# Graph attention on one core: windows of 128 nodes that begin at a group's first target, with the running maximum and sums kept for the window alone and scattered to memory

## The reference, cut to what matters

```python
z = h @ W.T
e = leaky_relu((z @ w1)[src] + (z @ w2)[dst], 0.01)
m = segment_max(e, dst)
num = exp(e - m[dst])
den = segment_sum(num, dst)
w_e = rel_emb[etype] * num / den[dst]
h_agg = segment_sum(w_e[:, None] * z[src], dst)
x = layernorm(x + h_agg + bias_w)
```

## Time and profile before

| | us |
|---|---|
| median of 3 runs (lowest, highest) | 9428.82 (9421.71, 9435.07) |
| profiled execution, device time | 9424.09 |
| its span | 9422.5 |
| attention stage, first to last row_scale (line 1046) | 3241.9 to 5041.8 |

### The profile page before, as it was taken

One profiled execution on the slowest core, in us unless ns is written; L12 is line 12 of the kernel. 1 busy time (PEld: TensorE's weight loads), 2 busy tenths in 40 slices (PEclk: granted clock), 3 DMA queues, 4 the chain that ended last, 5 costly groups with the idle time before them and its releaser, 6 DMA issues. The chain is left out here.

```text
span 9422.5 us, 155371 instructions
## 1 busy us (share of the span) xinstructions
PE 7624.8 (81%) x38400; PEld 4762.1 (51%) x38401; DVE 4037.7 (43%) x9289; ACT 3255.1 (35%) x5403; POOL 5567.4 (59%) x5492
## 2 busy tenths in 40 slices
PE   1998888888888576666667999999999888888886
PEld 1554444444444366555554444444444655566664
DVE  5887777774444366666654110000011332332333
ACT  4012334565555476666552000000000332332332
POOL 4888788877777010000003666676766677777775
PEclk6999999999999766666667999999999999999998
DMA  4233445566666443333325999999998322322222
GB/s 121 75 105 123 150 162 177 201 231 219 212 223 224 160 145 129 118 112 106 99 93 197 332 322 345 337 334 337 330 339 289 94 78 76 78 78 78 78 77 67
DMA packets 563155, 1661.17 MB, mean 176 GB/s; under 512 B 115314, under 2 KB 312030, under 8 KB 519495
## 3 DMA queue, kind: packets, MB, share of 16 engines
q1 hardware_dynamic: 352666, 1182.75, 35.8%
q0 software_dynamic: 206976, 473.99, 16.9%
q10 hardware_dynamic: 3312, 1.94, 0.1%
HBM read 1174.46 MB, written 483.82 MB: 176 GB/s over the span
## 5 line engine op out<-in xcount | busy, mean ns | idle before, releaser
L913 PE MATMUL wide<-ring 128*128 128x392 bf16 x14112 | 2501.0, 339 | 496.2 <-DVE ring L843 259.5
L520 POOL DMA_INDIRECT z_got<-z_table,z_idx x1568 | 2113.4, 1348 | 597.6 <-issue 430.2
L913 PEld LDWEIGHTS wide<-ring 128*128 128x128 bf16 x14112 | 1408.5, 100 | 1588.5 <-issue 820.9
L1672 POOL DMA_INDIRECT sorted_recs<-dn_rec_in,type_f x1568 | 1512.1, 964 | 735.2 <-issue 444.9
L1763 POOL DMA_INDIRECT l_rows<-h_table,l_recs x1568 | 1558.6, 994 | 520.1 <-issue 477.5
L1487 PE MATMUL wide<-stream,X 128*128 128x512 f32 (+1 forms) x2548 | 1048.1, 571 | 23.5 <-DVE X L1613 17.8
L1046 POOL TENSOR_TENSOR row_scale<-rows,rel 128x8 f32<-128x8 f32 x196 | 38.9, 198 | 1451.2 <-ACT m_scale L1150 1451.2
L1206 PE MATMUL wide<-rows,onehot 128*128 128x130 f32 x3904 | 845.0, 403 | 42.7 <-issue 21.1
L373 PE MATMUL wide<-l_rows,l_onehot 128*128 128x128 f32 x3904 | 579.3, 310 | 366.6 <-DVE X L386 366.6
L1206 PEld LDWEIGHTS wide<-rows,onehot 128*128 128x128 f32 x3904 | 788.0, 308 | 91.8 <-issue 91.5
L1862 DVE TENSOR_TENSOR l_rows<-l_filters,l_rows 128x1024 f32<-128x1024 f32 x196 | 240.3, 1226 | 1327.9 <-DMA l_rows<-h_table,l_recs 1310.5
(11 more groups left out here) (262 smaller groups left out, 8640.2 us busy)
## 6 DMA issues: line engine op xcount, KB each, us to landing
stream<-w_dense SPq DMA_DIRECT2D x252, 1792.0 KB, 9.5
stream<-c_dense SPq DMA_DIRECT2D x84, 1792.0 KB, 9.2
z_edges<-z_got POOLq DMA_DIRECT2D x196, 528.0 KB
rows<-z_edges POOLq DMA_DIRECT2D x196, 528.0 KB
dst_bc<-in_dst_row SPq DMA_DIRECT2D x196, 512.0 KB, 3.6
c_dense<-A SPq DMA_DIRECT2D x49, 1568.0 KB
w_dense<-A SPq DMA_DIRECT2D x49, 1568.0 KB
c_dense<-H SPq DMA_DIRECT2D x49, 1568.0 KB
```

The source lines that it names most:

```text
L520: e.indirect_dma_start(out=z_got[:, s, t, :], out_offset=None, in_=z_table, in_offset=bass.IndirectOffsetOnAxis(ap=z_idx[:, s, t:t + 1], a ...
L913: ins = e.matmul(banks[:, bass.ds(to[v], 1), int(m > 0), 0:WC].rearrange("p a x -> p (a x)"), lhsT=slots[:, k, m * P:(m + 1) * P], rhs=slo ...
L1672: e.indirect_dma_start(out=sorted_recs, out_offset=bass.IndirectOffsetOnAxis(ap=pos_i[:, g * TILES + t:g * TILES + t + 1], axis=0), in_=re ...
```

## The change

A group's window now begins at its first target `lo` and holds the nodes lo to lo + 127, node n still on partition n mod 128. The partitions below `lo mod 128` then stand for nodes of the next block. The end of a group's range becomes first + ((largest - lo + 128) >> 7).

- The prelude also stores each group's `lo` and broadcasts it to all partitions (`lo_f`); from it come the masks `below` and `above`.
- `node_tab` holds for each block the node's far value, its own score and the score's three parts. GpSimd (`describe`), two groups ahead, builds a window's record in `win` from two neighbouring blocks of it, and `W_RESET`, which is negative and huge where the node on a partition changes from one window to the next.
- VectorE keeps the maximum in `max_was` and the sums in `kept`, one column and one row of 130 values a partition. The steps of both are exponentiated into `m_scale`, twice as wide as before.
- After each `add_pair` GpSimd (`put_sums`) scatters `kept` by an indirect DMA to `agg_dram`, at rows made from the window's far value. VectorE adds to `kept` again only when that scatter has landed (`s_kept`).
- `agg_dram` is filled with zeros at the start on ScalarE's queue, which also loads `iota` now. The targets `dst_f` are turned into keys on VectorE.
- The dense stage loads `A0` from `agg_dram` by 7 DMAs on SyncE's queue ahead of its first stream load, and takes `rden` and `rdeg` slice by slice.

```diff
@@ attention, GpSimd
+                made, flushed = counter(e, "l0_pool_made", 1), counter(e, "l0_pool_flushed")
+                was, done = e.alloc_register("l0_pool_was"), counter(e, "l0_pool_done", 1)
+                landed, added = counter(e, "l0_pool_landed"), counter(e, "l0_pool_added")
+                regs = [range_registers(e, f"l0_pool{s}") for s in range(SLOTS)]
+
...
+                def describe(g, s, lo, hi):
+                    up, down = (m[:, g if isinstance(g, slice) else bass.ds(g, 1)].to_broadcast([P, 5]) for m in (above, below))
+                    with e.Fori(lo, hi) as b:
+                        e.reg_add(was, made, -1)
+                        now = bass.ds(e.snap(made, min_val=1, max_val=WINS - 1), 1)
+                        ahead_of = bass.ds(e.snap(was, min_val=0, max_val=WINS - 2), 1)
+                        to, reset = flat(win[:, now, 0:5]), flat(win[:, now, W_RESET:W_RESET + 1])
+                        e.tensor_tensor(to, flat(node_tab[:, bass.ds(b, 1), :]), up, ALU.mult)
+                        e.tensor_tensor(wrapped[:, :], flat(node_tab[:, bass.ds(b + 1, 1), :]), down, ALU.mult)
+                        e.drain()
+                        e.tensor_tensor(to, to, wrapped[:, :], ALU.add)
+                        e.drain()
+                        e.tensor_tensor(reset, flat(win[:, now, W_FAR:W_FAR + 1]),
+                                        flat(win[:, ahead_of, W_FAR:W_FAR + 1]), ALU.subtract)
+                        e.drain()
+                        e.tensor_tensor(reset, reset, far_off[:, :], ALU.mult)
+                        e.drain()
+                        e.tensor_copy(m_step[:, s, 1, bass.ds(b, 1)], reset).then_inc(s_win, 1)
+                        e.reg_add(made, made, 1)
+
+                def put_sums(first=False):
+                    if not first:
+                        e.reg_add(flushed, done, -2)
+                        e.wait_ge(s_added, added)
+                        e.sem_inc(note["pool"], 1)
+                    at = e.snap(flushed, min_val=0, max_val=WINS - 1)
+                    e.tensor_copy(node_far[:, :], flat(win[:, bass.ds(at, 1), W_FAR:W_FAR + 1]))
+                    e.drain()
+                    e.tensor_scalar(node_now[:, :], node_far[:, :], -1.0 / FAR, None, ALU.mult).then_inc(s_row, 1)
+                    e.wait_ge(s_row, done)
+                    e.sem_inc(note["pool"], 1)
+                    e.indirect_dma_start(out=agg_dram, out_offset=bass.IndirectOffsetOnAxis(ap=node_now[:, 0:1], axis=0),
+                                         in_=kept[:, :], in_offset=None).then_inc(s_kept, 16)
+                    e.reg_mov(added, done)
+                    e.reg_add(done, done, 1)
+                    e.reg_add(landed, landed, 16)
...
+                for g in range(2):
+                    load_range(e, table_dst, g, regs[g])
+                    describe(slice(g, g + 1), g, *same_range(e, regs[g]))
+                e.reg_mov(regs[-1][0], 0)
+                e.reg_mov(regs[-1][1], 1)
+                e.wait_ge(s_fill, 16)
+                put_sums(first=True)
                 with e.Fori(0, TURNS) as i:
                     for s in range(SLOTS):
                         g = i * SLOTS + s
+                        if s:
+                            put_group(*same_range(e, regs[s - 1]))
+                        else:
+                            with e.If(i > 0):
+                                put_group(*same_range(e, regs[-1]))
+                        if s < SLOTS - 2:
+                            load_range(e, table_dst, g + 2, regs[s + 2])
+                            describe(g + 2, s + 2, *same_range(e, regs[s + 2]))
...
+                        else:
+                            with e.If(i < TURNS - 1):
+                                e.reg_mov(ahead, i * SLOTS + (s + 2))
+                                after = e.snap(ahead, min_val=0, max_val=NG - 1)
+                                load_range(e, table_dst, after, regs[s + 2 - SLOTS])
+                                describe(after, s + 2 - SLOTS, *same_range(e, regs[s + 2 - SLOTS]))
...
+                put_group(*same_range(e, regs[-1]))
+                put_sums()
+                e.wait_ge(s_kept, landed)
+                e.sem_inc(note["pool"], 1)
@@ attention, SyncE and ScalarE
-                e.dma_start(dst_f[:, :].bitcast(i32), T["dst_c"]).then_inc(s_iota, 16)
-                e.dma_start(iota[:, :], T["iota"].to_broadcast([P, NP_])).then_inc(s_iota, 16)
+                e.dma_start(dst_f[:, :].bitcast(i32), T["dst_c"]).then_inc(s_dst, 16)
...
+                        e.reg_add(w, w, 1)
+                        e.wait_ge(s_win, w)
...
+                e.dma_start(iota[:, :], T["iota"].to_broadcast([P, NP_])).then_inc(s_iota, 16)
+                e.wait_ge(s_zero, 1)
+                e.dma_start(agg_dram.rearrange("(b p) f -> p b f", p=P),
+                            zeros[:, :].unsqueeze(1).to_broadcast([P, NB + 1, SW_])).then_inc(s_fill, 16)
...
-                        e.activation(m_scale[:, s * NB:(s + 1) * NB], m_step[:, k, :], ACT.Exp).then_inc(s_num, 1)
+                        e.activation(m_scale[:, s * 2 * NB:(s + 1) * 2 * NB], m_step[:, s, :, :].rearrange("p a b -> p (a b)"),
+                                     ACT.Exp).then_inc(s_num, 1)
@@ attention, VectorE before its loop
+                e.memset(zeros[:, :], 0.0)
+                e.memset(m_step[:, :, :, :], 0.0)
+                e.memset(kept[:, :], 0.0)
+                e.drain().then_inc(s_zero, 1)
...
+                e.wait_ge(s_dst, 16)
+                dst_i = dst_f[:, :].bitcast(i32)
+
+                def of_group(per_group):
+                    return per_group[:, :].unsqueeze(2).to_broadcast([P, NG, TILES])
+
+                def by_group(per_edge):
+                    return per_edge.rearrange("p (g t) -> p g t", t=TILES)
+
+                e.tensor_tensor(by_group(key_i), by_group(dst_i), of_group(lo_f), ALU.subtract)
+                e.tensor_scalar(low_i, dst_i, P - 1, None, ALU.bitwise_and)
+                e.drain()
+                e.tensor_scalar(key_i, key_i, 7, 7, ALU.arith_shift_right, ALU.logical_shift_left)
+                e.tensor_tensor(by_group(low_i.bitcast(f32)), by_group(low_i), of_group(lo_block), ALU.add)
+                e.drain()
+                e.tensor_tensor(dst_f[:, :], key_i, low_i.bitcast(f32), ALU.add)
@@ attention, VectorE add_pair and sums
-                    b = e.snap(last_b, min_val=0, max_val=NB - 1)
-                    scale = e.snap(last_scale, min_val=0, max_val=SLOTS * NB - 1)
+                    scale = e.snap(last_scale, min_val=0, max_val=(2 * SLOTS - 1) * NB - 1)
                     new = flat(pair_sums[:, bass.ds(e.snap(other, min_val=0, max_val=1), 1), :])
-                    to, deg = A[:, bass.ds(b * SW_, MW)], A[:, bass.ds(b * SW_ + MW, 1)]
-                    e.scalar_tensor_tensor(out=to, in0=to, scalar=m_scale[:, bass.ds(scale, 1)], in1=new[:, 0:MW],
-                                           op0=ALU.mult, op1=ALU.add)
-                    e.tensor_tensor(deg, deg, new[:, MW:SW_], ALU.add)
+                    e.reg_add(landed, landed, 16)
+                    e.wait_ge(s_kept, landed)
+                    e.sem_inc(note["dve"], 1)
+                    e.scalar_tensor_tensor(out=kept[:, 0:MW], in0=kept[:, 0:MW], scalar=m_scale[:, bass.ds(scale, 1)],
+                                           in1=new[:, 0:MW], op0=ALU.mult, op1=ALU.add)
+                    e.scalar_tensor_tensor(out=kept[:, MW:SW_], in0=kept[:, MW:SW_], scalar=m_scale[:, bass.ds(scale + NB, 1)],
+                                           in1=new[:, MW:SW_], op0=ALU.mult, op1=ALU.add).then_inc(s_added, 1)
 
                 def sums(g, s, lo, hi):
+                    e.wait_ge(s_iota, 16)
                     e.wait_ge(s_num, g + 1)
                     e.sem_inc(note["dve"], 1)
                     with e.Fori(lo, hi) as b:
@@ -1283,8 +1433,7 @@
                                 add_pair(e)
                             half_onehot(e, h, b, dst_f[:, bass.ds(g * TILES + 4 * h, 4)].unsqueeze(2)
                                         ).then_inc(half_ready[h], 1)
-                        e.reg_mov(last_b, b)
-                        e.reg_mov(last_scale, b + s * NB)
+                        e.reg_mov(last_scale, b + s * 2 * NB)
 
@@ attention, VectorE per window
                         with e.Fori(lo, hi) as b:
                             e.reg_add(c, c, 1)
+                            e.reg_add(w, w, 1)
+                            at = e.snap(w, min_val=1, max_val=WINS - 2)
+                            e.drain()
                             e.wait_ge(s_away, c)
                             e.wait_ge(s_sbc, g + 2)
                             e.sem_inc(note["dve"], 1)
                             e.tensor_tensor_reduce(out=hid[:, :], in0=s_rowed[k], in1=away[:, :],
```

(53 more changed lines are left out.)

120 lines of the change are left out of this document (82 added, 38 removed).

## The result

The change makes the kernel slower: 9877.64 us (median of 4, 9874.83 to 9880.36) against 9425.26 us (median of 4), ratio 1.0479 with a 95% interval of 1.0464 to 1.0495. The forecast was 9100 us.

What follows compares the result with a forecast made beforehand. ScalarE and VectorE were taken as both full at 6.85 us a group, GpSimd nearly empty. 9424.1 - 464 + 118 + 14 = 9092 us, forecast as 9100 us, range 9000 to 9320.

Steps and rivals of the forecast that it cites:

- What goes: Attention stage: all 196 groups get one window and the 48 second windows go, -464 us.
- The period no longer drifts: Sign in the attention stage: one row_scale every 7.45 us from first group to last; drift would mean a wrong forecast.
- The ring: Attention loop: add_pair, put_sums, describe, max_was, one-hot, add_pair takes 7.45 us a group against 6.85, +118 us; chance 0.40.
- Each microsecond costs 196 us: Attention loop: from about 4.4 us of GpSimd work a group, each further microsecond adds 196 us to the run.
- What GpSimd gets: GpSimd's new work per group after add_pair: put_sums 2.7 us and describe 2.25 us, together 4.95 us.
- 0.15 us for the drain between: Term of put_sums: a GpSimd drain between the copy and the index conversion, 0.15 us.
- 0.18 us for drain and restart: Term of describe: each of five dependent GpSimd steps takes 0.38 us, 0.20 us plus 0.18 us for drain and restart.
- The bounds: GpSimd's new work per group: between 4.0 and some 8.8 us, the upper end giving a ring of 11.3 us.
- slower: Rival: put_sums and describe take over 6.7 us, the ring over 9.15 us a group; chance 0.07.
- s_kept hidden: Attention loop: add_pair's wait for the last scatter's landing, 4.4 us against 7.45, costs nothing.
- The lock: VectorE-GpSimd port sharing: scatter starts after the second one-hot, so nothing charged; if every scatter met one, +135 us.
- Once per run: Outside the attention loop: start 0, last scatter's landing +4, dense stage +9, prelude +1 us, together +14 us.

Runs made afterwards that it cites:

- e_early: Changed kernel with semaphore waits for its loop drains, early table loads and zero fill, and scatter indices made before the wait for VectorE's addition: 9079.7 us, ratio 0.9628.
- e_order: Changed kernel with semaphore waits in place of all loop drains and describe ahead of put_sums: 9174.7 us, ratio 0.9737, period 7.78 us.
- e_both: Changed kernel with all five loop drains made semaphore waits, same order, on another chip: 10185.2 us, ratio 0.9766 to the kernel before, period 7.69 us.
- e_orderd: Changed kernel with all drains kept and only describe moved ahead of put_sums: 9404.78 us, period 8.97 us.
- e_last: e_early with describe and row_scale both moved ahead of put_sums: 9212.33 us, ratio 0.977, period 8.06 us.
- e_best: e_order with table loads waited for where used, zero fill issued in the first stage, and a semaphore wait for the start's drain: 9149.14 us, ratio 0.9709.
- e_earlyo: e_early with describe moved ahead of put_sums: 9157.5 us, period 7.80 us.
- e_bdrain: Kernel before with a GpSimd drain right behind each load of rows, on another chip: attention stage 1797.2 us.
- e_put: Changed kernel with only put_sums' drain made a semaphore wait, on another chip: 10354.74 us, attention stage 1693.6 us, period 8.69 us.

## Why the prediction was wrong

Set against the trace in spans, the forecast was 9422.5 - 464 + 118 + 14 = 9090.5 us; 9873.3 came, 782.8 us more. Of these 769.5 us lie in the attention stage (2223.4 instead of 1453.9), 22.6 us ahead of it (23.6 instead of 1), and -9.4 us behind it (3.6 instead of 13).

- **What goes: right.** One window in every group, hid 196 times, no wait of VectorE for TensorE ahead of a one-hot. The period no longer drifts. e_early's stage is 358 us shorter than the one before: the 464 us less 0.54 us for each of 195 periods.
- **The ring: right in mechanism and place for this kernel.** max_was waits for describe's last copy in 193 groups, and ScalarE waits for row_scale. With the drains out, a turn in which it waits takes 7.42 us in two groups of four and 7.59 us in a third, where 7.45 was forecast. The mean is 7.69 us, 1499 us of stage where 1454 was forecast, because the fourth group is longer without that wait. At that length the ring is no longer the only limit: e_order cut it and stayed at 7.78 us. "Each microsecond costs 196 us" holds only roughly: GpSimd's two steps got 4.2 us shorter in e_both and the period 3.7 us.
- **What GpSimd gets: the step that failed.** Two terms, "0.15 us for the drain between" in put_sums and "0.18 us for drain and restart" per step of describe, were taken from VectorE's spacing and row_scale's length. They hold for a drain with no DMA of GpSimd in flight (0.15 to 0.27 us between two steps). The first drain of each half stood behind one: 2.20 instead of 0.15, and 2.40 instead of 0.18 us, 4.3 us a turn. The sum of the turn goes from 7.45 to 11.7 with these two; 11.54 was measured.
- **The other terms of it held.** Copy to be started 0.27 us after the addition (0.4 forecast), the gap ahead of the DMA 0.84 us (0.79), its descriptors 1.11 us (0.97), VectorE's part 2.32 us (2.52). Of its terms, the 0.05 us for the signal stands in no row; in the trace the signal follows the copy's end by 0.01 us, and max_was starts 0.37 us after that end.
- **The bounds missed it as well.** The upper end, a ring of 11.3 us, came out near the truth, but by terms that did not occur (small instructions of 0.59 us). The rival "slower" had the right threshold, over 9.15 us, and the wrong reason; its 0.07 came from weighing only those. The trace of before has no drain of GpSimd between two steps of its attention loop, and a wait that the trace does not show there was costed by the row it looked like. It has long ones elsewhere, 13.2 us at 175.7 us with gathers under way and 7.1 us at the attention stage's end; they could have warned, and no row of the prediction has them.
- **s_kept hidden: right here** (1.5 us, once), and it becomes a wait as soon as the scatter leaves later (e_orderd, e_order, e_last).
- **The lock.** The scatter met no one-hot, as forecast. But the copy did: it starts at 4011.99 and ends at 4012.37, with VectorE's second one-hot from 4011.63 to 4012.32, and takes 0.38 us. Its median is 0.38 us in the kernel after, where it meets a one-hot in every turn, and 0.18 us in e_order, where it meets none. That is 0.2 us a group which the sum left out; the 7.42 us of e_both hold it, so other terms came out shorter. The Trainium skill says, in SBUF — State Buffer, Who interferes with whom, that a VectorE instruction with two inputs in SBUF contends with a GpSimd instruction that reads SBUF. The trace agrees, with these 0.38 us; the rule does not explain the drains.
- **Once per run.** The start was forecast at 0 (ends -8 and +12) and the prelude at +1. The prelude gave +10.9 us, since the table's load waits for two more stores of one column (issued at 41.4 instead of 30.5 us), and the start the other 12.7 us, with the drain of 18.2 us and the wait for the fill. e_best regains 22.3 us of both. Behind the stage 13 us were forecast and 3.6 came: the first matmul of the dense stage comes 32.6 us after the last row_scale instead of 24.0 us, and part of that is regained after.

The landing of a DMA was in the prediction's rows all along (2.6 us for a gather). It was charged to add_pair, where a semaphore names it, and not to the drain, where nothing does.

## What to carry to other kernels

In these kernels a drain on the queue that issues DMAs from GpSimd is at least a wait for their landing: count each at what the last DMA still has to go, or let a small instruction signal a semaphore and wait for that. When work is put on an idle engine, look at what it is put behind in that engine's queue; two steps of some 0.2 us became 2.2 and 2.4 us by their place. And where a step is both waited for by two engines and followed by a landing that a third needs, the order in the queue is a choice to be measured: e_early, e_earlyo and e_last hold the same steps, and their periods of 7.39, 7.80 and 8.06 us differ by order alone. A mean period can also hide a group that another limit sets, as the fourth of each loop turn here.

## What the runs showed of the hardware

- A drain of GpSimd directly behind its load of 528 KB ends 3.88 us after the load's start, the wait for the load's landing semaphore 3.86 us after it. Each drain in e_bdrain ends 0.07 to 0.08 us after the load's last landing signal. Behind a small compute instruction with no DMA in flight a drain takes 0.24 to 0.28 us (medians).
- At the stage's end, with all DMAs of GpSimd landed, its drain takes 6.03 to 7.07 us in kernels with no drain in the loop and 0.05 to 0.40 us in those with one in every turn. The reason is not shown.
- A copy of GpSimd (128x1) takes 0.38 us where a one-hot of VectorE with two inputs in SBUF runs at the same time, 0.18 us where none does.
- Between a compute instruction of GpSimd and an indirect DMA that uses its result 0.83 to 0.87 us pass (medians), whether a drain or a semaphore orders the steps ahead of it.
- A wait on a semaphore that GpSimd's own instruction raises costs 0.19 to 0.29 us between two small dependent instructions, no more than the drain with nothing in flight.
- The same scatter does not always land after the same time: its last signal comes 3.54 us after its start in the kernel after and 2.71 us in e_put (medians). What makes the difference is not shown.
